# Two attention blocks on one core: value and output weights kept apart, keys for four pairs at once, and a new instruction order

## Chip, core and metric

The kernel runs on one core of a Trainium2 chip. The metric is the device time of one execution in microseconds (us), as the median of several executions. TensorE (PE), VectorE (DVE), ScalarE (ACT), GpSimd (POOL) and SyncE (SP, which issues the DMAs) each run their own instruction stream in order, and hand over to one another with semaphores.

## What is computed

`x` and the context `c` are 32 sequences of 64 tokens by 128 features. Block 0 has causal self-attention, cross-attention and a feed-forward layer, each followed by a layer norm, with 16 heads of width 8. Block 1 is cross-attention with 16 heads of width 64 and a given bias `f` that is added twice.

```python
def _mha(x, kv, Wq, Wk, Wv, mask, causal):       # block 0, width 8 per head
    energy = jnp.einsum('bhsk,bhtk->bhst', Q, K)
    lengths = jnp.sum(energy[:, :, 0, :] != 0, axis=-1)
    energy = jnp.where(cols >= lengths[:, :, None, None], -jnp.inf, energy)
    ...
    score = softmax(energy / sqrt(dk)); out = score @ V * m
# block 1, width 64 per head
qh, kh, vh = q @ wq + bq, c @ wk + bk, c @ wv + bv
weights = softmax(qh @ kh.T / 8 + f + f)
out = LN((weights @ vh) @ wo + bo + q)
```

## The kernel before

**Tiling.** Two sequences make a pair, 2 x 64 tokens on the 128 partitions, so there are 16 pairs. Each pair goes through three chains. Chain A is the self-attention and norm L1. Chain B is the cross-attention and norm L2, then the feed-forward layer and norm L3. Chain C is block 1 and norm L4. A works three or four pairs ahead of C and B two, so that in a full round all three chains have a pair in work.

**PSUM.** Each chain of block 0 has three banks: J (projections), E and X (scores, transposed weights, results). Chain C has two, `C.E[0]` and `C.E[1]`, through which everything of a pair passes in turn: transposed input, queries, scores, keys and values of a later pair, transposed weights, output, and then the input of the next pair.

**Chain C, step by step (before).** `C.x3t`/`C.x3ts` transpose and copy the input; `C.q_0/1` compute the queries in two halves of eight heads and `C.qs_0/1` (ACT, four instructions each) copy them out with bias and scale; `C.e` computes the scores (32 small matmuls); `C.fadd` (DVE) adds the bias `f`; `C.max` (DVE), `C.sub` (POOL), `C.exp` (ACT), `C.den` (DVE, sum and reciprocal) and `C.nrm` (DVE, the normalising product in place in `Pc`) are the softmax; `C.pt`/`C.pts` transpose and copy it; `C.o` multiplies by `VW` and `C.y` adds the residual. `C.k`/`C.ks` make the keys of one pair (8 matmuls 128x128; DVE adds the bias), and `C.v`/`C.vs` make the values. Before, the values are already multiplied by the output weights: at the start `C.fold` computes Wv[h] Wo[h] for all heads and splits it into two parts, so `C.v` is 12 matmuls of 512 columns in a faster number format (fp32r), and four DMAs (`C.vz`) bring the halves into place as `VW`.

**Chains A and B** have the same steps with their own names: `qkv`, `qk`, `q0`, `e0`, `nz`, `cnt`, `cut`, `kblk` (POOL, 128x1024), `e`, `max`, `sub`, `exp`, `pt`, `pts`, `pv`, `zts`, `z`, `zn`, `y`, `st`, `rstd` (POOL), `xh`, `gb` (POOL).

**Order.** A table written by hand, `TURN`, lists every step with the pair that it is ahead by. Each engine walks through the table once per round and issues the steps that are its own; the functions `run` and `body` do that. What an engine issues is thus fixed, and a step that waits holds up all that stands behind it on its engine. A full round does one pair of each chain.

Of the kernel before, what the change touches and what calls it, by code (L numbers as in the profile page):

```python
# [75 lines left out]
def bass_two_blocks(nc, consts, columns, x, xT, ctxn, ctxT, fs, Wq1, Wk1, Wv1, Wq2, Wk2, Wv2, fc1T, fc2T,  # L76
                    vecs, fc1b, wq, wk, wvT, wo, bq, bk, bv, out):
    with ExitStack() as stack:
# [23 lines left out]
        wvT_sb, wo_sb = sb("wvT_sb", [P, J, D]), sb("wo_sb", [P, J, D])  # L102
        wvo_hi, wvo_lo = sb("wvo_hi", [P, 2, 2, J // 2, D], F32R), sb("wvo_lo", [P, 2, 2, J // 2, D], F32R)
# [21 lines left out]
        def attention(name):  # L125
# [9 lines left out]
            a.V = [sb(name + f"_V{k}", [P, 2, H, SLOT]) for k in range(2)]  # L135
# [3 lines left out]
            a.zn = sb(name + "_zn", [P, D])  # L139
# [911 lines left out]
```

## Time and profile before

| | us |
|---|---|
| median of 3 runs | 418.62 (417.07 to 419.54) |
| the profiled execution, its own time | 419.26 |
| span of its instructions | 417.5 |
| busy in the span: PE, DVE, ACT, POOL | 367.7, 345.4, 225.9, 218.4 |

A profile row is one instruction, or several alike in a row: start, duration, engine, line of the kernel, operation, output <- inputs, count, and in brackets the idle time of the engine before it with what ended it. An fp32 matmul is recorded as two instructions, one for each pass over the moving columns. Since matmuls are pipelined, the duration of a record runs into the next one; what a group costs PE is the distance from its start to the start of the next group.

### The profile page before, as it was taken

Reading aid. Unit: us, or ns where it says so; the run is one execution under the profiler, and the core shown is the slowest. Engines: PE = TensorE matmul, PEld = TensorE weight load, DVE = VectorE, ACT = ScalarE, POOL = GpSimd, SP = SyncE. Lnnn points to the kernel's source line nnn. Section 1 sums busy time; section 2 is a strip of 40 time slices with the busy share of each in tenths; the row PEclk is TensorE's granted clock in tenths of the full one; section 3 lists DMA queues with packets and bytes.
Section 4 is the critical chain, followed back from the end, with each engine's and each line's share of the span. In section 5 each row is a group of like instructions: output and inputs, shape, how many; then the busy total and the mean of one; then the engine's idle time right before and its main releaser. Section 6 shows DMA issues by size and latency. Waiting matters only on the chain.

```text
span 417.5 us, 12301 instructions
## 1 busy us (share of the span) xinstructions
PE 367.7 (88%) x4816; PEld 282.1 (68%) x4816; DVE 345.4 (83%) x895; ACT 225.9 (54%) x549; POOL 218.4 (52%) x356
## 2 busy tenths in 40 slices
PE   2488779899999999999999999999999989998834
PEld 1355547677777786868686868686877767766633
DVE  3146586899999999999999999999999999695751
ACT  1022344666675666656665666576666575645431
POOL 0013244555747566565656565666575746554531
PEclk9999989999999999999999999999999999999996
DMA  6980000314141423224150504141414141414040
GB/s 193 308 328 2 2 0 16 88 52 105 58 102 58 95 61 82 80 54 108 27 134 9 128 33 104 59 103 58 103 59 104 57 104 60 102 58 102 6 104 13
DMA packets 15801, 34.61 MB, mean 83 GB/s; under 512 B 2560, under 2 KB 7936, under 8 KB 15616
## 3 DMA queue, kind: packets, MB, share of 16 engines
q1 hardware_dynamic: 15744, 33.83, 30.3%
q8 instruction: 38, 0.62, 0.7%
q14 instruction: 19, 0.16, 0.1%
HBM read 15.99 MB, written 1.05 MB: 41 GB/s over the span
## 4 chain that ended last, share of the span: by engine, by line
PE 47%; DVE 36%; issue 7%; ACT 3%; DMA 2%; POOL 2%; SPq 1%; POOLq 0%; DVEq 0%
DVE Pc L895 8%; PE C_E L509 7%; PE C_E L545 7%; PE C_E L521 4%; DVE denc L885 4%; PE A_E L386 4%; DVE kT L855 4%; DVE mxc L877 4%; DVE Sc L868 3%; PE C_E L532 2%; PE A_J L350 2%; DMA wo_sb<-in_wo 2%; PE B_E L419 2%; PE B_E L405 2%; PE C_E L315 2%
## 5 line engine op out<-in xcount | busy, mean ns | idle before, releaser
L938 POOL TENSOR_TENSOR L_ve<-L_mv,cst 128x1 f32<-128x1 f32 x64 | 12.1, 189 | 77.9 <-DVE L_mv L822 77.8
L949 POOL TENSOR_TENSOR L_xg<-L_xh,vec_sb 128x128 f32<-128x128 f32 x64 | 35.0, 547 | 32.2 <-DVE L_xh L831 32.2
L930 POOL TENSOR_TENSOR A_kblk<-A_qk,cst 128x1024 f32<-128x1024 f32 x16 | 30.3, 1896 | 34.1 <-DVE A_qk L755 34.1
L978 POOL TENSOR_TENSOR Sc<-Sc,mxc 128x512 f32<-128x512 f32 x32 | 33.4, 1043 | 24.0 <-DVE mxc L877 24.0
L643 ACT COPY vst<-C_E 128x512 f32<-128x512 f32 x64 | 37.6, 587 | 4.3 <-PE C_E L490 4.1
L657 ACT ACTIVATE qT<-C_E,bq 128x128 f32<-128x128 f32 x128 | 36.2, 366 | 5.6 <-PE C_E L509 5.6
L930 POOL TENSOR_TENSOR B_kblk<-B_qk,cst 128x1024 f32<-128x1024 f32 x16 | 30.4, 1897 | 15.5 <-DVE B_qk L755 15.5
L940 POOL TENSOR_TENSOR L_rstd<-L_ve,cst 128x1 f32<-128x1 f32 x64 | 35.1, 548 | 5.0
L509 PE MATMUL C_E<-x3T,wq_sb 128*128 128x128 f32 x256 | 36.8, 287 | 0.4 <-ACT x3T L649 0.4
L474 PE MATMUL C_E<-cTs,wk_sb 128*128 128x128 f32 x256 | 35.6, 282 | 1.3 <-DVE Sc L868 1.3
L895 DVE TENSOR_TENSOR Pc<-Pc,rdc 128x512 f32<-128x512 f32 x32 | 36.1, 1128 | 0.7
L545 PEld LDWEIGHTS C_E<-VW,PTc 128*64 128x64 f32 x512 | 29.0, 142 | 9.3 <-ACT PTc L674 8.9
L590 ACT ACTIVATE B_S<-B_S 128x512 f32<-128x512 f32 x32 | 20.2, 630 | 27.4 <-DVE B_S L789 26.9
L474 PEld LDWEIGHTS C_E<-cTs,wk_sb 128*128 128x128 f32 x256 | 31.0, 191 | 4.3 <-issue 2.6
L674 ACT COPY PTc<-C_E 128x512 f32<-128x512 f32 x32 | 18.4, 586 | 28.4 <-PE C_E L532 28.4
L509 PEld LDWEIGHTS C_E<-x3T,wq_sb 128*128 128x128 f32 x256 | 30.9, 191 | 4.1 <-ACT x3T L649 2.4
L545 PE MATMUL C_E<-VW,PTc 128*64 128x128 f32 x512 | 32.9, 284 | 0.7 <-ACT PTc L674 0.7
L532 PEld LDWEIGHTS C_E<-cst,Pc 128*128 128x128 f32 x128 | 14.1, 145 | 27.7 <-DVE Pc L895 18.0
L532 PE MATMUL C_E<-cst,Pc 128*128 128x128 f32 x128 | 21.2, 294 | 12.8 <-DVE Pc L895 12.3
L488 PE MATMUL C_E<-wvo_hi,cT_hi 128*128 128x512 f32 x64 | 29.2, 457 | 0.2 <-DVE kT L855 0.2
L868 DVE SCALAR_TENSOR_TENSOR Sc<-f,C_E 128x512 f32<-128x512 f32 x32 | 21.8, 681 | 8.0 <-PE C_E L521 8.0
L665 ACT ACTIVATE Pc<-Sc 128x512 f32<-128x512 f32 x32 | 20.4, 638 | 10.3 <-POOL Sc L978 10.3
(149 smaller groups left out, 1047.8 us busy)
## 6 DMA issues: line engine op xcount, KB each, us to landing
VW<-vst SPq DMA_DIRECT2D x64, 256.0 KB, 4.4
f<-in_fs SPq DMA_DIRECT2D x16, 512.0 KB, 3.5
cTs<-in_ctxT SPq DMA_DIRECT2D x1, 1024.0 KB, 6.6
out<-osb SPq DMA_DIRECT2D x16, 64.0 KB, 1.5
xTs<-in_xT SPq DMA_DIRECT2D x1, 960.0 KB, 8.3
vec_sb<-in_vecs SPq DMA_DIRECT2D x1, 640.0 KB, 4.3
wvT_sb<-in_wvT SPq DMA_DIRECT2D x1, 512.0 KB, 8.1
wo_sb<-in_wo SPq DMA_DIRECT2D x1, 512.0 KB, 9.3
```

The costliest lines, as they stand in the source:

```text
L474: last = mm(C.E[g][:, j * P:(j + 1) * P], wk_sb[:, c:c + P], cols(cTs, n), start=True, stop=True)
L509: last = mm(C.E[g][:, j * P:(j + 1) * P], wq_sb[:, c:c + P], x3T[:], start=True, stop=True)
L532: last = tr(C.E[g][:, j * P:(j + 1) * P], Pc[:, c:c + P], ident)
L545: last = mm(C.E[0][S * b:S * b + S, 0:D], PTc[:, c:c + S], VW[:, b, j], start=(j == 0), stop=(j == J - 1), skip_group_check=True)
L643: act.copy(vst[:, m // 2, 4 * (m % 2):4 * (m % 2) + 4].rearrange("p j d -> p (j d)"), C.E[m % 2][:, :]).then_inc(C.s_vs, 1)
L657: last = act.activation(qT[:, 4 * g + j], C.E[g][:, j * P:(j + 1) * P], ACT.Identity, bias=bq8[:, 4 * g + j:4 * g + j + 1], scale=float(DK ...
L868: dve.scalar_tensor_tensor(sc, f[n % 2][:, g * HALF:(g + 1) * HALF], 2.0, C.E[g][:, :], ALU.mult, ALU.add).then_inc(C.s_s, 1)
L895: tt(pr, pr, rdc[:, 8 * g:8 * g + 8].unsqueeze(2).to_broadcast([P, 8, S]), ALU.mult).then_inc(C.s_nrm, 1)
L930: tt(a.kblk[:], a.qk[:, 1].unsqueeze(1).to_broadcast([P, 8, P]), at["rmask"].unsqueeze(2).to_broadcast([P, 8, P]), ALU.mult).then_inc(a.s_ ...
L940: tt(l.rstd[:], l.ve[:], at["power"], ALU.pow).then_inc(l.s_rstd, 1)
L949: tt(l.xg[:], l.xh[:], l.g, ALU.mult).then_inc(l.s_xg, 1)
L978: tt(v, v, mxc[:, 8 * g:8 * g + 8].unsqueeze(2).to_broadcast([P, 8, S]), ALU.subtract).then_inc(C.s_sub, 1)
```

## The change

1. Wv and Wo are not folded. `C.fold`, its copies (`fhi`, `flo`), `C.chi` and `C.clo` and the four DMAs per pair are gone. `C.v` computes plain values in fp32 (4 matmuls with 64 stationary and 512 moving columns), ACT copies them with 2 instructions instead of 4. New steps: `C.zt` (32 matmuls 64x64x64: weights times values, transposed), `C.zts` (2 ACT copies of 128x512), and `C.o` (8 matmuls 128x128x128 with Wo).
2. Keys are computed for four pairs at once: `C.k` of pair n does two of the eight key blocks of a group of four pairs (2 matmuls with 512 moving columns), five rounds ahead. The bias is added by ACT (`C.ks`), not DVE.
3. In A and B each partition half keeps only the values of its own heads: the projection's value part has 64 columns instead of 128, and `v` on DVE becomes two narrow and two 64x128 instructions per pair and chain instead of one 128x32 and one 128x256.
4. `zn` and the sums `y` (L1, L2, L3, `ffn`) lie in PSUM. The score matmuls of the next pair therefore wait for `xh` of the pair before, no longer for `zn`; `B.tr` waits for L3's `xh`. `q0` and `cut` read PSUM.
5. `C.nrm` runs on POOL.
6. The loads at the start come in another order and in pieces (first four pairs of x and c, then the weights, then the rest). `C.bvo`, the product of Wo with the value bias, stands before the second `A.qkv` on PE.
7. `TURN` is a new table. (A table `SHIFT` that could delay single pairs holds zeros only.)

```diff
-                sp.dma_start(t[:], ap.rearrange("(j p) d -> p j d", p=P)).then_inc(w_fold, 16)
+            load_x(0, 0, FIRST)
...
+            sp.dma_start(wo_sb[:], wo.rearrange("(j p) d -> p j d", p=P)).then_inc(w_out, 16)
+            sp.dma_start(bv_sb[:], bv).then_inc(w_out, 16)
...
-                        sp.dma_start(VW[S * m:S * m + S, b], vst[S * b:S * b + S, m]).then_inc(C.s_vz, 16)
...
-            def energy(a, causal):
+            def energy(a, l, causal):
...
-                        pe.wait_ge(a.s_zn, 2 * n)
+                        pe.wait_ge(l.s_xh, n)
...
-                    for j in range(4):
-                        c = (4 * g + j) * P
-                        last = mm(C.E[g][:, j * P:(j + 1) * P], wk_sb[:, c:c + P], cols(cTs, n), start=True, stop=True)
+                    mm(C.E[g][:, :], wk_sb[:, j * P:(j + 1) * P], cTs[:, group * FIRST * P:(group + 1) * FIRST * P],
+                       start=True, stop=True).then_inc(C.s_k, 1)
...
-                    mm(bank[:, :], cT_hi[:], hi, start=True, stop=False)
-                    mm(bank[:, :], cT_hi[:], lo, start=False, stop=False)
-                    mm(bank[:, :], cT_lo[:], hi, start=False, stop=True).then_inc(C.s_v, 1)
+                    for r in range(2):
+                        last = mm(C.E[b][S * r:S * r + S, :], cTs[:, n * P + S * b:n * P + S * b + S], wv_sb[:, r],
+                                  start=True, stop=True)
...
+            def c_zt(n):
+
+                pe.wait_ge(C.s_pts, 2 * n + 2)
+                for jj in range(J // 2):
+                    for b in range(2):
+                        c = jj * P + S * b
+                        for hl in range(2):
+                            for r in range(2):
+                                k = slice(S * r, S * r + S)
+                                v = jj * P + DK1 * hl
+                                last = mm(C.E[r][DK1 * hl:DK1 * hl + DK1, c:c + S], V[n % 2][k, b, v:v + DK1],
+                                          PTc[k, hl * HALF + c:hl * HALF + c + S], start=True, stop=True)
...
+                    pe.wait_ge(C.s_zts, 2 * n + 1 + r)
+                    for jj in range(J // 2):
+                        last = mm(C.E[0][:, 0:D], zT[:, r, jj], wo_sb[:, 2 * jj + r], start=(r == jj == 0),
+                                  stop=(r == 1 and jj == J // 2 - 1))
...
-            def nrm(g):
-
-                def step(n):
-                    dve.wait_ge(C.s_rd, 2 * n + 1 + g)
...
+            def nrm(g):
+
+                def step(n):
+                    pool.wait_ge(C.s_rd, 2 * n + 1 + g)
+                    pr = heads(Pc[:, g * HALF:(g + 1) * HALF])
+                    tt(pr, pr, rdc[:, 8 * g:8 * g + 8].unsqueeze(2).to_broadcast([P, 8, S]),
+                       ALU.mult).then_inc(C.s_nrm, 1)
```

**PE at the start.** Before, from the first projection on; `wo_sb,wvT_sb` is the fold:

```order
L350 MATMUL A_J<-Wv_sb,xTs 64x128 x4
L315 MATMUL C_E<-wo_sb,wvT_sb 128x128 x4
L360 MATMUL A_J<-A_q,A_qk 64x16 x2
L315 MATMUL C_E<-wo_sb,wvT_sb 128x128 x4
L372 MATMUL A_J<-A_nz,ofb 128x16 x2
L374 MATMUL A_J<-ofb,A_nz 128x2
L315 MATMUL C_E<-wo_sb,wvT_sb 128x128 x4
L386 MATMUL A_E<-A_kblk,A_qk 64x512 x2
```

After:

```order
L326 MATMUL A_J<-Wv_sb,xTs 64x64 x4
L336 MATMUL A_J<-A_q,A_qk 64x16 x2
L348 MATMUL A_J<-A_nz,ofb 128x16 x2
L350 MATMUL A_J<-ofb,A_nz 128x2
L302 MATMUL C_E<-wo_sb,bv_sb 128x128 x8
L321 MATMUL A_J<-xTs,Wq_sb 128x128
L322 MATMUL A_J<-xTs,Wk_sb 128x128
L326 MATMUL A_J<-Wv_sb,xTs 64x64 x4
L362 MATMUL A_E<-A_kblk,A_qk 64x512 x2
```

The small steps of the first pair no longer stand behind the fold; the eight matmuls with `bv_sb` (before, in front of the third `A.qkv`) now stand in front of the second `A.qkv` and the first scores.

**PE in a full round, from the second half of the queries (`x3T,wq_sb`) to the scores (`kT,qT`) of chain C.** Before:

```order
L509 MATMUL C_E<-x3T,wq_sb 128x128 x4
L430 MATMUL B_X<-cst,B_zT 128x128 x2
L345 MATMUL A_J<-xTs,Wq_sb 128x128
L346 MATMUL A_J<-xTs,Wk_sb 128x128
L350 MATMUL A_J<-Wv_sb,xTs 64x128 x4
L442 MATMUL B_J<-cst,x_1 128x128
L443 MATMUL B_J<-cst,cm 128x128
L521 MATMUL C_E<-kT,qT 64x64 x32
```

After, with what follows the scores:

```order
L488 MATMUL C_E<-x3T,wq_sb 128x128 x4
L321 MATMUL B_J<-xc,Wq_sb 128x128
L322 MATMUL B_J<-xc,Wk_sb 128x128
L326 MATMUL B_J<-Wv_sb,xc 64x64 x4
L501 MATMUL C_E<-kT,qT 64x64 x32
L321 MATMUL A_J<-xTs,Wq_sb 128x128
L322 MATMUL A_J<-xTs,Wk_sb 128x128
L326 MATMUL A_J<-Wv_sb,xTs 64x64 x4
L336 MATMUL B_J<-B_q,B_qk 64x16 x2
L362 MATMUL A_E<-A_kblk,A_qk 64x512 x2
```

Less work stands between the queries and the scores, and the projection and the scores of chain A have moved behind the scores of chain C.

**POOL in a full round, around the softmax of chain C (`Sc,mxc` is `C.sub`).** Before:

```order
L978 TENSOR_TENSOR Sc<-Sc,mxc 128x512 x2
L930 TENSOR_TENSOR B_kblk<-B_qk,cst 128x1024
L949 TENSOR_TENSOR L_xg<-L_xh,vec_sb 128x128
L954 TENSOR_TENSOR osb<-L_xg,vec_sb 128x128
L930 TENSOR_TENSOR A_kblk<-A_qk,cst 128x1024
```

After:

```order
L932 TENSOR_TENSOR Sc<-Sc,mxc 128x512 x2
L891 TENSOR_TENSOR B_kblk<-B_qk,cst 128x1024
L941 TENSOR_TENSOR Pc<-Pc,rdc 128x512 x2
L910 TENSOR_TENSOR L_xg<-L_xh,vec_sb 128x128
L915 TENSOR_TENSOR x_1<-L_xg,vec_sb 128x128
```

The two normalising products stand directly behind `B.kblk`.

## Rows read from the trace of the kernel before

**Rows 1.** The page's chain that ended last: share of the span by engine.
```profile
PE 47%; DVE 36%; issue 7%; ACT 3%; DMA 2%; POOL 2%; SPq 1%; POOLq 0%; DVEq 0%
```
**Rows 2.** Busy time by engine in one full round: stretch, length, then each engine.
```profile
180.80:202.80 22.00, 21.38 (x299) 16.55 (x299) 21.09 (x56) 13.85 (x35) 13.66 (x22) 1.00 0.31 77
```
**Rows 3.** Timeline of PE in that round: start, duration, what.
```profile
181.43 0.65 PE L386 MATMUL A_E<-A_kblk,A_qk 64*64 64x512 f32 x2
...
182.34 0.38 PE L393 MATMUL A_E<-later,eye 64*64 64x512 bf16 x2
...
182.67 1.97 PE L545 MATMUL C_E<-VW,PTc 128*64 128x128 f32 x32
...
190.20 1.16 PE L521 MATMUL C_E<-kT,qT 64*64 64x64 f32 x64
191.29 0.49 PE L345 MATMUL B_J<-xc,Wq_sb 128*128 128x128 f32 x2
...
191.93 0.66 PE L350 MATMUL B_J<-Wv_sb,xc 128*64 128x128 f32 x8
192.52 1.16 PE L474 MATMUL C_E<-cTs,wk_sb 128*128 128x128 f32 x8
193.61 0.29 PE L360 MATMUL A_J<-A_q,A_qk 128*64 128x16 f32 x4
...
194.44 1.06 PE L474 MATMUL C_E<-cTs,wk_sb 128*128 128x128 f32 x8
195.34 0.60 PE L405 MATMUL A_X<-cst,A_S 128*128 128x128 f32 x4
...
195.86 0.48 PE L488 MATMUL C_E<-wvo_hi,cT_hi 128*128 128x512 f32 x1
...
197.35 0.23 PE L372 MATMUL A_J<-A_nz,ofb 128*128 128x16 bf16 x2
...
202.80 0.33 PE L532 MATMUL C_E<-cst,Pc 128*128 128x128 f32 x1 [0.57 <-DVE Pc L895]
```
**Rows 4.** Single lines over the whole run: count, duration ns min/median/max.
```profile
L895 DVE TENSOR_TENSOR Pc<-Pc,rdc x32: 681/1036/1480, 88.9 to 407.1; 128x512 f32<-128x512 f32 x32
...
L978 POOL TENSOR_TENSOR Sc<-Sc,mxc x32: 1038/1043/1048, 83.9 to 404.2; 128x512 f32<-128x512 f32 x32
```
**Rows 5.** The page's groups by line: busy us, mean ns | idle before them.
```profile
L930 POOL TENSOR_TENSOR B_kblk<-B_qk,cst 128x1024 f32<-128x1024 f32 x16 | 30.4, 1897 | 15.5 <-DVE B_qk L755 15.5
L643 ACT COPY vst<-C_E 128x512 f32<-128x512 f32 x64 | 37.6, 587 | 4.3 <-PE C_E L490 4.1
...
L868 DVE SCALAR_TENSOR_TENSOR Sc<-f,C_E 128x512 f32<-128x512 f32 x32 | 21.8, 681 | 8.0 <-PE C_E L521 8.0
```
**Rows 6.** Timeline of PE in a later round, chain A nearly done: queries to scores.
```profile
361.20 1.16 PE L509 MATMUL C_E<-x3T,wq_sb 128*128 128x128 f32 x8
362.20 0.39 PE L430 MATMUL B_X<-cst,B_zT 128*128 128x128 f32 x2
...
363.59 1.16 PE L521 MATMUL C_E<-kT,qT 64*64 64x64 f32 x64 [0.65 <-ACT qT L657]
```
**Rows 7.** Timeline of PE at the start.
```profile
16.47 2.07 PE L315 MATMUL C_E<-wo_sb,wvT_sb 64*128 64x128 f32 x8 [9.33 <-DMA wo_sb<-in_wo]
...
24.36 1.12 PE L386 MATMUL A_E<-A_kblk,A_qk 64*64 64x512 f32 x2
...
39.77 3.68 PE L326 MATMUL C_E<-wo_sb,bv_sb 128*128 128x128 f32 x16
43.28 0.39 PE L345 MATMUL A_J<-xTs,Wq_sb 128*128 128x128 f32 x2
```
**Rows 8.** Timeline of PE: queries of the first and the thirteenth pair; the last output.
```profile
76.23 1.16 PE L509 MATMUL C_E<-x3T,wq_sb 128*128 128x128 f32 x8
...
339.40 1.16 PE L509 MATMUL C_E<-x3T,wq_sb 128*128 128x128 f32 x8
...
408.90 3.38 PE L545 MATMUL C_E<-VW,PTc 128*64 128x128 f32 x32
```

More of the change, by code:

```diff
@@ L134, in attention @@
             a.S = sb(name + "_S", [P, H * S])
-            a.V = [sb(name + f"_V{k}", [P, 2, H, SLOT]) for k in range(2)]
+            a.V = [sb(name + f"_V{k}", [P, 2, J, 2, SLOT]) for k in range(2)]
             a.PT = sb(name + "_PT", [P, H * S])
@@ L224, in bass_two_blocks @@
         C.s_pts = sem("C_pts")
+        C.s_zt = sem("C_zt")
+        C.s_zts = sem("C_zts")
         C.s_o = sem("C_o")
@@ L231, in run @@
         def run(steps):
-            def body(i):
-                for chain, step, ahead in ORDER:
-                    fn = steps.get(chain + "." + step)
-                    n = i + ahead
-                    if fn and 0 <= n < PAIRS:
-                        fn(n)
-            for i in range(-AHEAD, PAIRS):
-                body(i)
+            for _, chain, step, n in PLAN:
+                fn = steps.get(chain + "." + step)
+                if fn:
+                    fn(n)
         def cols(t, n):
@@ L301, in _ @@
             mm, tr = nc.tensor.matmul, nc.tensor.transpose
-            def fold(part):
-                def step(n):
-                    if n:
-                        return
-                    hl, q = part // 2, part % 2
-                    if part == 0:
-                        pe.wait_ge(w_fold, 16 * 2)
-                    if part >= 2:
-                        pe.wait_ge(wvo_split, part - 1)
-                    r = slice(DK1 * hl, DK1 * hl + DK1)
-                    for j in range(4):
-                        last = mm(C.E[q][:, j * P:(j + 1) * P], wvT_sb[r, 4 * q + j], wo_sb[r, 4 * q + j],
-                                  start=True, stop=True)
-                    last.then_inc(wvo_ready, 1)
-                return step
             def bvo(n):
@@ L521, in c_e @@
                             last = mm(C.E[hl][S * b:S * b + S, j * S:(j + 1) * S], qT[r, j, S * b:S * b + S],
-                                      kT[r, j, S * b:S * b + S], start=True, stop=True)
+                                      keys[r, j, S * b:S * b + S], start=True, stop=True)
                 last.then_inc(C.s_e, 1)
@@ L1005 @@
-C.v_2+2 B.3xh+2 B.sub_1+3 A.pts_0+4 B.f2+2 A.z+4 A.y+4 A.pts_1+4 C.exp_0+1 C.v_3+2 C.gb+0 B.f3+2 C.vs_0+2
-C.fhi_3+4 C.exp_1+1 B.e+3 A.kblk+5 C.y+1 A.zts+4 B.f1s+2 A.st+4 C.pt_0+1 C.flo_3+4 C.pt_1+1 B.3rstd+2 C.vs_1+2
-C.fold_2+5 B.3gb+2 C.x3c+2 C.obias+3 C.st+1 A.rstd+4 B.f2s+2 C.flo_0+5 A.e+5
-"""
-ORDER = [(w[0], w[2:].split("+")[0], int(w.split("+")[1])) for w in TURN.split()]
-AHEAD = max(k for _, _, k in ORDER)
+B.pv_0+2 C.den_0+1 B.gb+2 C.qs_1+1 C.den_1+1 C.sub_0+1 A.sub_0+5 B.qk+3 B.pv_1+2 A.qk+6 C.ks_0+5 C.bvo+5 C.q_0+1
@@ new lines @@
+A.cnt+6 A.st+5 B.pts_0+3 B.pts_1+3 A.pt_1+5 C.gb+0 B.zn+3 B.y+3 C.zt+1 C.x3ts+2 B.st+3 B.q0+4 B.xts+4 C.xh+1
+A.pv_0+5 A.pv_1+5 B.pt_0+3 B.zts+3 A.xh+5 B.xh+3 C.o_0+1 C.o_1+1 C.rstd+1 C.fadd_0+2 A.rstd+5 B.pt_1+3 C.max_0+2
+B.nz+4 B.tr+4 C.obias+6 C.loadf+5 B.rstd+3 C.qs_0+2 A.z+5 C.fadd_1+2 C.max_1+2 C.store+4 B.cut+4 A.max_0+6
+C.x3t+2 A.q0+7 B.v+4
+"""
+SHIFT = """
+A 0 0 0 0 0 0 0 0 0 0 0 0 0 0 0 0
+B 0 0 0 0 0 0 0 0 0 0 0 0 0 0 0 0
+C 0 0 0 0 0 0 0 0 0 0 0 0 0 0 0 0
+"""
+WORDS = TURN.split()
@@ L1012 @@
+LATER = {r[0]: [float(v) for v in r[1:].split()] for r in SHIFT.strip().split("\n")}
+PLAN = sorted((n + k / len(WORDS) - int(w.split("+")[1]) + LATER[w[0]][n], w[0], w[2:].split("+")[0], n)
+              for k, w in enumerate(WORDS) for n in range(PAIRS))
 _OUT = ((B, S, D), "float32")
```

350 lines of the change are left out of this document (158 added, 192 removed).

## Prediction

> **What bounds the kernel now.** I read the chain of waits first. It is nearly all PE and DVE, with POOL at 2% and DMA at 2% [rows 1], so neither engine alone sets the end: work goes back and forth between the two. The busy times of one full round say how close both are to their limit: PE 21.4 us and DVE 21.1 of 22.0, ACT 13.9, POOL 13.7 [rows 2]. The queries of the first pair start on PE at 76.23 us and those of the thirteenth at 339.40 [rows 8], so twelve full rounds take 263.2 us, 21.93 each. What is left is the head (76.2 us) and the tail (417.5 - 339.4 = 78.1 us). In a full round PE stands still in one place for 0.57 us, before the second half of the transposed weights, and it is DVE's normalising product that releases it (the last of [rows 3]). PE's own work is thus 21.93 - 0.57 = 21.36 us per round. This is the number that the change has to lower; relief on DVE alone is worth at most the 0.57.
>
> **The full round, part by part (PE, from start to start).**
>
> Keys: before 1.09 + 0.90 = 1.99 us (192.52 to 193.61 and 194.44 to 195.34 in [rows 3]). The price of an fp32 matmul with 512 moving columns is that of the score matmuls of chain A, where four tiles stream side by side, each two passes, in 182.34 - 181.43 = 0.91 us. Two of them are 1.82: -0.2.
>
> Values: six of the twelve fp32r matmuls take 197.35 - 195.86 = 1.49 us, so all twelve some 3.0. After there are four fp32 matmuls of 512 columns, two and two side by side in the column halves: 2 x 0.91 = 1.8, so -1.2. If the two didn't overlap it would be 3.6, +0.6 (a rival, below). That narrow tiles do overlap is shown by the output product: 32 records of 128 columns in 1.9 us are 59 ns each, and the keys, the same columns over the full width, need 1.09/8 = 136 ns.
>
> Value part of the projections in A and B: 192.52 - 191.93 = 0.59 us each for 128 columns; half the columns, -0.3 each, -0.6 (nothing, if the 64 columns were bounded by something else).
>
> New `C.zt`: 32 matmuls of 64x64x64 in four tiles, like the scores of chain C, 191.29 - 190.20 = 1.09: +1.1. `C.o`: before 1.9; after eight matmuls of 128 columns, priced as queries (four in 1.00, [rows 6]) or keys (four in 1.09): 2.1, +0.2.
>
> The sum is -0.2 - 1.2 - 0.6 + 1.1 + 0.2 = -0.7, PE's work becomes 20.7 us (20.4 to 21.3 with terms at their milder ends, leaving out the rival).
>
> DVE loses the two key copies and the two products (0.68 and a mean of 1.13 us each by their lines, 3.6 per round) and gets some 0.4 for the split value steps: about 17.9 us. It drops well below PE, and that cost is hidden. ACT loses two copies of 0.59 [rows 5], the small cast, and gains two key copies and two `zts`: about +1, 15 us, hidden by its 8 us of idleness as a sum, not at each place. The four DMAs per pair land early and nobody on the chain waits for them; nothing.
>
> **Where PE waits now.** Two places, both new. (a) Between the second half of the queries and the scores of C, ACT must finish eight small copies. In a round where PE has too little else, the scores start 363.59 - 361.20 = 2.39 us after that half starts, 0.65 of it waited [rows 6]. The new order leaves the projection of B between them: 1.09 + (191.29 to 192.52, 1.23, less 0.3) = 2.0 us. So PE waits 0.4. (b) Transposed weights: from the end of the scores DVE does two additions and two maxima at 0.68 and one small step (2.9 us), then POOL in its order one more subtraction at 1.04, `B.kblk` at 1.90 and two products. A product on POOL has the form and size of the subtraction, min 1038 and max 1048 ns [rows 4]: 2.1. That is 7.9 us to the release. Meanwhile PE has the projection and scores of A (0.9 + 1.2), keys and values (3.6), the scores of B (0.9), small groups (an estimate, 0.9) and the first transposes (0.6): 8.1. It just fits, with 0.2 to spare. The longer hold of the banks in A and B (the scores wait for `xh`) costs nothing: on DVE `xh` stands just ahead of C's additions, so it is done when C's scores end; A's next scores stand 1.1 us later on PE, B's about 6. So the round is 20.7 + 0.4 = 21.1 us, and twelve of them give 12 x (21.1 - 21.93) = **-10.0 us**. What is late next is (a), a handful of ACT copies, and directly behind it (b).
>
> A rule that speaks against (b): [rows 4] show the product on DVE at 0.68 us alone and 1.48 us at worst, beside POOL, and POOL's 512-wide subtraction at 1.04 whatever DVE does. The Trainium skill, GPSIMD Engine Reference, section 3.1, gives an fp32 `tensor_tensor` on GpSimd as 1.96 times slower than on DVE; that would make each product 1.3 us, use up the spare time and lengthen the round by 0.4, 5 us over twelve rounds. The trace's 1.04 is for the same shape and is what I take. The same skill, SBUF — State Buffer, "Who interferes with whom", says that a DVE instruction with two SBUF inputs contends with GpSimd; moving the product away ends this for DVE's largest such instruction, and the 0.68 against 1.48 agrees.
>
> **Head.** Before, PE waited until 16.47 us for `wo_sb` and ran four fold groups of 2.07 each; the first scores stood at 24.36 [rows 7]. After, the same wait holds `bvo`, which is now second in line, and `wo_sb` stands behind more bytes and more DMA issues: I take 19 us (16.5 to 21). Then 3.6 for `bvo` and some 2.3 for a projection at the slow rate (twice its 1.2) give 25 for the first scores, +0.7. The 3.5 us of `bvo` at 39.77 to 43.28 are gone from there. PE ran its matmuls slowly until 43.28: a pair of score records takes 1.12 us at 24.36 and 0.65 in the full round [rows 7, 3]; right behind `bvo` it ran at the full rate (0.39 for two projection records). If `bvo` brings that about at 25 already, the pieces of 20 us that follow are shorter, some 4 us; the three rounds of the head are set by latency, not by PE's sum, so I count 1. The head is **-3.7 us** (-8 to +3).
>
> **Tail.** With A gone, the path of one pair through C sets the pace. It gets `zt` (1.1) and a copy (0.6, the second one is hidden by the first output matmuls) for four pairs, 4 x 1.7 = 6.8, and for the last pair at the slow rate 1.1 more (the last output at 408.90 took 3.38, not 1.9 [rows 8]). Against that, the keys have left the last three rounds (2.0 each on PE) and the values are shorter (I count 0.4 of their 1.2): 3 x 2.4 = 7.2. **+0.7 us** (-4 to +5).
>
> Sum: -10.0 - 3.7 + 0.7 = -13.0. The profiled execution took 419.26 us with a span of 417.5; so 406.3 for it, and 405.6 against the median of 418.62. I say 406.
>
> **Rivals.**
>
> R1, slower: POOL becomes the pacemaker of the round. All that stands behind `B.kblk` is released by it, and there is only 0.2 us to spare. If a product on POOL takes twice the 1.04, in conflict with DVE as DVE's did (rows 4: 681 to 1480 ns for one instruction), the round is 21.1 + 2.1 - 0.2 = 23.0: 12 x 1.07 - 3 = +10, about **428 us**. It decides from a round of 22.2, that is from 1.7 us per product. Against it: the POOL rows don't vary. 12%.
>
> R2, the same: the two value matmuls of a half don't overlap, or a wait of one us arises on ACT (its queue puts key copies before the exponentials). Round 22.0, head -3: **416 us**. 10%.
>
> R3, more: PE runs at its full rate from the first 25 us, which takes 8 us from the head, and (a) doesn't bind, so that the round is PE's 20.7 or less: -8 - 15 + 1 = -22, **397 us**. 17%.
>
> R4, less: the loads keep `bvo` to 21 us or beyond and the deeper staging of A before B makes the head 3 us longer; the round is right: **412 us**. 15%.
>
> My own sum, 401 to 410: 46%. Faster by over 0.5% (which is about what a measurement of this kernel can tell from no change, 2 us) is then 46 + 17 + 15 and a part of R2: 0.80; the same 0.07; slower 0.13. The range leaves out R1 and the end of R3: 394 to 419.
>
> **What the profile after would show.** Distance of the first query matmuls from pair to pair: 21.1; over 22 refutes the sum. PE's work per group: keys and values 1.8 each, `zt` 1.1, `o` 2.1. POOL's product at 1.04, and PE's wait before the transposes under 0.2 us; a wait of over 1 us released by POOL is R1. PE's idle time before the scores of C 0.4, released by ACT. At the start `bvo` at 19 us and the first scores of A at 25, the first queries of C at 72 to 73. DVE busy at most 18 us per round. The prediction is wrong if ACT or POOL show up in the chain of waits with more than a few per cent.

## The result, and the profile after

| us | before | after |
|---|---|---|
| median (20 executions each) | 417.67 | 415.00 |
| lowest to highest | 413.48 to 419.64 | 412.68 to 417.83 |
| the profiled execution, its span | 419.26, 417.5 | 412.68, 410.8 |
| busy: PE, DVE, ACT, POOL | 367.7, 345.4, 225.9, 218.4 | 347.7, 309.3, 235.4, 236.2 |

The ratio of the times is 0.9933, with a 95% interval of 0.9907 to 0.9958. The change makes the kernel 2.7 us faster; 13 were forecast. The profiled execution of after is the fastest of its 20, that of before is 1.6 us slower than its median, so the two traces differ by 6.7 us where the medians differ by 2.7.

The page's chain that ended last, after, for [rows 1]:

```profile
PE 65%; ACT 15%; DVE 8%; issue 4%; POOL 3%; SPq 3%; DMA 2%; POOLq 0%; DVEq 0%
```

PE has taken DVE's place. A full round is as [rows 2] show it for before. Busy time by engine, then the granted clock, from the queries of one pair to those of the next:

```profile
179.39:200.38 20.99, 20.50 (x337) 14.47 (x331) 19.44 (x59) 14.44 (x36) 14.73 (x25) 1.00 0.09 30
```

The same round on PE's timeline, for [rows 3]; one wait is left in it, before the scores of C:

```profile
181.50 0.39 PE L321 MATMUL B_J<-xc,Wq_sb 128*128 128x128 f32 x2
...
182.90 1.16 PE L501 MATMUL C_E<-kT,qT 64*64 64x64 f32 x64 [0.40 <-ACT qT L644]
183.99 0.49 PE L321 MATMUL A_J<-xTs,Wq_sb 128*128 128x128 f32 x2
...
186.42 1.96 PE L453 MATMUL C_E<-cTs,wk_sb 128*128 128x512 f32 x4
188.32 1.08 PE L467 MATMUL C_E<-wv_sb,cTs 128*64 128x512 f32 x4
189.43 0.30 PE L426 MATMUL B_J<-cst,x 128*128 128x128 f32 x1
...
189.80 1.06 PE L467 MATMUL C_E<-wv_sb,cTs 128*64 128x512 f32 x4
190.79 0.65 PE L362 MATMUL B_E<-B_kblk,B_qk 64*64 64x512 f32 x2
...
192.13 1.04 PE L512 MATMUL C_E<-cst,Pc 128*128 128x128 f32 x8
...
194.52 1.16 PE L526 MATMUL C_E<-PTc,C_V 64*64 64x64 f32 x64
195.62 0.69 PE L395 MATMUL A_E<-A_PT,A_V 128*32 128x64 f32 x32
...
196.73 1.95 PE L535 MATMUL C_E<-wo_sb,C_zT 128*128 128x128 f32 x16
198.52 0.60 PE L381 MATMUL B_X<-cst,B_S 128*128 128x128 f32 x4
```

Keys take 1.90 us, the values 1.11 and 0.99, `zt` 1.10 and `o` 1.79. POOL in the same round: the products follow `B.kblk`, and the second ends at 192.40, while the eight transposes start at 192.13, so that their second half starts about 0.2 us behind it:

```profile
188.12 1.90 POOL L891 TENSOR_TENSOR B_kblk<-B_qk,cst 128x1024 f32<-128x1024 f32 x1
190.36 2.04 POOL L941 TENSOR_TENSOR Pc<-Pc,rdc 128x512 f32<-128x512 f32 x2 [0.34 <-DVE rdc L859]
```

By stages, from the queries of the first and the thirteenth pair ([rows 8] for before; after they start at 74.43 and 325.97):

| us | before | forecast | after, profiled | difference |
|---|---|---|---|---|
| head | 76.2 | -3.7 | 74.4 | -1.8 |
| twelve rounds | 263.2 | -10.0 | 251.5 | -11.6 |
| tail | 78.1 | +0.7 | 84.8 | +6.7 |

The tail alone takes back more than half of what the rounds give. The page's clock row of after shows where; a slice is 10.3 us, and the digits below 9 all stand in the last eight slices, from 329 us on:

```profile
PEclk9999999999999999999999999999999978999866
```

In windows of 10 us, columns as in [rows 2]:

```profile
330.00:340.00 10.00, 6.80 (x70) 2.31 (x63) 7.01 (x19) 2.48 (x5) 7.71 (x9) 0.73 0.17 54
...
350.00:360.00 10.00, 6.36 (x105) 3.24 (x105) 7.75 (x22) 4.04 (x11) 7.11 (x9) 1.00 0.17 54
...
390.00:400.00 10.00, 3.73 (x88) 2.80 (x82) 4.43 (x8) 2.43 (x4) 5.45 (x7) 0.63 0.02 7
400.00:410.00 10.00, 4.94 (x60) 4.45 (x53) 1.11 (x4) 1.07 (x2) 1.64 (x4) 0.67 0.03 8
```

Before had 1.00 in every such window from 330 to 400 us. PE's timeline of after tells what it did: it waited, and the groups behind the waits ran at the lower of the clock's two levels, 1.2 and not 2.4 GHz.

```profile
332.37 0.23 PE L348 MATMUL B_J<-B_nz,ofb 128*128 128x16 bf16 x2 [1.51 <-DVE B_nz L719]
335.31 0.45 PE L426 MATMUL B_J<-cst,x 128*128 128x128 f32 x1 [1.70 <-DVE B_V L752]
...
380.22 1.99 PE L526 MATMUL C_E<-PTc,C_V 64*64 64x64 f32 x64 [0.25 <-ACT PTc L661]
...
396.06 1.11 PE L512 MATMUL C_E<-cst,Pc 128*128 128x128 f32 x4 [5.39 <-POOL Pc L941]
...
399.17 1.99 PE L526 MATMUL C_E<-PTc,C_V 64*64 64x64 f32 x64 [0.68 <-ACT PTc L661]
401.86 3.79 PE L535 MATMUL C_E<-wo_sb,C_zT 128*128 128x128 f32 x16 [0.70 <-ACT C_zT L631]
```

By their rows `zt` takes 1.99 and not 1.16, `o` 3.79 and not 1.95 as in the full round.

### The profile page after: what moved, and what is told of

It is laid out like the page before. It is cut to its first block, busy times and chain, and to the rows that moved or that the text cites. A ratio compares the mean times of both kernels' runs of the same rounds, so it can differ in the third digit from the quotient of the medians.

```text
span 410.8 us, 13138 instructions
## 1 busy us (share of the span) xinstructions
PE 347.7 (85%) x5296; PEld 242.4 (59%) x5296; DVE 309.3 (75%) x897; ACT 235.4 (57%) x561; POOL 236.2 (57%) x372
## 4 chain that ended last, share of the span: by engine, by line
PE 65%; ACT 15%; DVE 8%; issue 4%; POOL 3%; SPq 3%; DMA 2%; POOLq 0%; DVEq 0%
ACT qT L644 8%; PE C_E L535 8%; PE C_E L453 6%; PE C_E L467 6%; PE C_E L526 5%; PE C_E L488 4%; PE C_E L501 4%; PE A_E L362 4%; PE B_E L362 3%; PE B_E L395 3%; ACT A_S L566 2%; PE C_E L512 2%; PE A_X L381 2%; ACT PTc L661 2%; PE A_E L395 2%
## 5 line engine op out<-in xcount | busy, mean ns | idle before, releaser
L559 ACT COPY A_qk<-A_J 128x256 f32<-128x256 f32 x16 | 6.0, 372 | 71.8 <-PE A_X L369 67.0
L467 PE MATMUL C_E<-wv_sb,cTs 128*64 128x512 f32 x128 | 35.2, 628 | 0.8 <-DVE Sc L840 0.8
L941 POOL TENSOR_TENSOR Pc<-Pc,rdc 128x512 f32<-128x512 f32 x32 | 32.8, 1042 | 5.3 <-DVE rdc L859 5.3
L535 PE MATMUL C_E<-wo_sb,C_zT 128*128 128x128 f32 x256 | 33.3, 286 | 1.6 <-ACT C_zT L631 1.4
L535 PEld LDWEIGHTS C_E<-wo_sb,C_zT 128*128 128x128 f32 x256 | 31.5, 200 | 2.5 <-ACT C_zT L631 2.5
L453 PE MATMUL C_E<-cTs,wk_sb 128*128 128x512 f32 x64 | 31.4, 614 | 0.0
L612 ACT ACTIVATE kT<-C_E,bk_sb 128x512 f32<-128x512 f32 x32 | 21.9, 683 | 15.0 <-PE C_E L453 15.0
L501 PE MATMUL C_E<-kT,qT 64*64 64x64 f32 x1024 | 18.6, 221 | 8.2 <-ACT qT L644 8.2
L622 ACT COPY C_V<-C_E 128x512 f32<-128x512 f32 x32 | 18.5, 583 | 10.8 <-PE C_E L467 10.8
L857 DVE TENSOR_REDUCE denc<-Pc 128x8 f32<-128x512 f32 x32 | 21.2, 663 | 2.2 <-ACT Pc L652 1.8
```

The costliest lines, as they stand in the source:

```text
L453: mm(C.E[g][:, :], wk_sb[:, j * P:(j + 1) * P], cTs[:, group * FIRST * P:(group + 1) * FIRST * P], start=True, stop=True).then_inc(C.s_k, 1)
L467: last = mm(C.E[b][S * r:S * r + S, :], cTs[:, n * P + S * b:n * P + S * b + S], wv_sb[:, r], start=True, stop=True)
L501: last = mm(C.E[hl][S * b:S * b + S, j * S:(j + 1) * S], qT[r, j, S * b:S * b + S], keys[r, j, S * b:S * b + S], start=True, stop=True)
L535: last = mm(C.E[0][:, 0:D], zT[:, r, jj], wo_sb[:, 2 * jj + r], start=(r == jj == 0), stop=(r == 1 and jj == J // 2 - 1))
L941: tt(pr, pr, rdc[:, 8 * g:8 * g + 8].unsqueeze(2).to_broadcast([P, 8, S]), ALU.mult).then_inc(C.s_nrm, 1)
```

## The experiments

All times are medians. Before was measured beside every group of runs and took 417.69, 417.87 and 417.93; a ratio is that to before, with its interval. A difference to after is one to its second median, 415.70. To fill PE's waits the runs use filler matmuls: work whose result nobody reads.

### The tail's clock

**Fillers in the tail.** The definition, and one of the seven places:

```diff
+            def fill(count):
+                for _ in range(count):
+                    mm(A.E[:, :], A.nz[:], eye64[:, :].unsqueeze(1).to_broadcast([P, 8, S]), start=True, stop=True)
...
+                    if n == 15 and g == 0:
+                        fill(21)
                     pe.wait_ge(C.s_nrm, 2 * n + 1 + g)
```

> The kernel after, with idle time of PE in the tail filled by matmuls that nobody reads (bf16, eye64 against A.nz into the free bank A.E, 0.2 us each): 6 before `B.cnt` and 5 before `C.e` of the last two pairs, 7 before `B.f1` of pairs 13 and 14, 10 before `B.f2`, 21 before the first transposes of the last weights, 2 before the last `zt`, 2 before each of the last `o`. In after the granted clock is 0.73 in the stretch from 330 to 340 us and 0.63 and 0.67 in the last 20 us, and groups at the low level take 1.8 to 2 times as long (values 1.98 instead of 1.08, zt 1.99 instead of 1.09, o 3.79 instead of 1.79). Theory (the low clock in the waits of the tail is a real part of its length): clock above 0.9 in these stretches, tail from the queries of the thirteenth pair to the end 84.8 - 4 to 6 us, total 3 to 6 us below the kernel after. Rival (the tail is bounded by the hand-overs between DVE, POOL and ACT, the slow groups only fill what would be waits): the clock rises but the total stays within 1 us, or grows by what the fillers cost where they don't quite fit.

409.11 us, ratio 0.9818 (0.977 to 0.9866). The tail takes 405.9 - 327.57 = 78.3 us, 6.5 less. The two windows that stood at 0.73 and 0.63:

```profile
330.00:340.00 10.00, 9.38 (x118) 4.31 (x116) 8.01 (x22) 3.97 (x11) 7.39 (x9) 1.00 0.17 54
390.00:400.00 10.00, 8.18 (x104) 4.85 (x103) 3.29 (x7) 3.50 (x6) 5.45 (x7) 1.00 0.03 9
```

There is more work on PE, and the tail is shorter. The rival, that slow groups only fill what would be waits, is refuted.

**After, unchanged, once more.**

> The kernel after, unchanged, on the chip and in the hour of the three runs beside it. The earlier loads gave 407.5 us by median and a span of 406.0, the fillers 409.1 and 405.9, y and zn in SBUF 410.6 and 410.1, against a median of 415.0 and a profiled span of 410.8 of the kernel after in another hour. If its median is 415 again (413.5 to 416.5), these differences are the edits' own, and the profiled execution of after (412.68, the fastest of 20) is an unusually short one. If it is 412 to 413, some 2.5 us of each difference is a matter of the chip or the hour, and y and zn in SBUF gain at most 2 us.

415.70 us (12 executions), ratio 0.9959 (0.9928 to 0.999), so the differences of the edits are their own. The profiled execution is a long one this time, span 415.8. Rounds (251.7) and tail (84.8) are those of the first profile, but the first queries stand at 79.25, not 74.43, and the clock tells why. The same three windows of the head, in this profile:

```profile
30.00:40.00 10.00, 6.88 (x71) 3.75 (x72) 5.27 (x17) 2.42 (x5) 3.55 (x5) 0.78 0.04 16
40.00:50.00 10.00, 8.71 (x70) 5.17 (x69) 5.33 (x18) 5.06 (x10) 2.27 (x3) 0.67 0.00 1
50.00:60.00 10.00, 8.32 (x77) 4.03 (x80) 7.17 (x19) 4.20 (x8) 3.14 (x4) 0.87 0.01 2
```

In the first profile they read 1.00. The waits are the same in both, and the groups are longer; the scores of A for the second pair stand at 35.90 with 0.65 us there, and here:

```profile
36.52 1.11 PE L362 MATMUL A_E<-A_kblk,A_qk 64*64 64x512 f32 x2 [2.38 <-DVE L_xh L811]
```

So two executions of one kernel differ in the head by 5 us, by the clock alone. The first profile is the rarer case: of the first 20 executions three had its mean granted clock of 0.969 and took 412.7 us, the other 17 had 0.952 to 0.965 and took 413.1 to 417.8. With the rounds and the tail as in both profiles, the median span of these 12 executions (413.9) leaves 77.4 us for the head of a typical one; that is worked out, not seen.

**Fillers in the last two pairs of before** (3 and 5 before `C.e`, 20 before the last transposes, 2 before the last `C.o`; the form is the same).

> The kernel before, with the same sort of filler matmuls in PE's waits of its last two pairs: 3 and 5 before `C.e`, 20 before the last transposes, 2 before the last output product. Before lost its clock only there (0.75 and 0.73 after 400 us), after lost it from 330 us on. Theory (the tail of after fails by the clock, that of before hardly did): before gains 1.5 to 3 us in all, since only the last transposes (1.1 to 0.65) and the last output product (3.4 to 1.9) are on the path at the low level, where the fillers gave 6 us to after; with the clock held in both, the tails differ by the term of the prediction, +0.7, to within 2 us. Rival (fillers give the same in both, so that the clock doesn't explain the difference of the two tails): before gains 5 us or more.

416.40 us, ratio 0.997 (0.9933 to 1.0008), so the medians alone can't tell it from no change. The tail is 410.5 - 333.86 = 76.6 us against 78.1, which is 1.5 less, as expected. With the clock held in both, the tails are 76.6 and 78.3, so the work and waits of the change cost 1.7 us there. Its profiled execution had its first queries at 70.47, those of before in [rows 8] 76.23, with not one filler in the head, so the head of before varies in the same way. The waits are the same up to there, but PE leaves its low level with the fourth fold group, where [rows 7] have it until 43.28:

```profile
27.00 1.16 PE L319 MATMUL C_E<-wo_sb,wvT_sb 64*128 64x128 f32 x8
...
70.47 1.16 PE L513 MATMUL C_E<-x3T,wq_sb 128*128 128x128 f32 x8
```

The stage table above thus compares a slow head of before with a fast one of after. The median span of before in its 23 executions beside these runs is 416.1; less the rounds (263.2) and the tail (78.1) that leaves 74.8 us, against the 77.4 of after. For typical executions the head did not get shorter by 1.8 us but longer by 2.6. This too is worked out, not seen.

**The clock held at both ends of after.**

```diff
+                early_fill(A.E, 45)
                 pe.wait_ge(w_out, 16 * 2)
...
+                    if a is A and n in (1, 2):
+                        early_fill(A.E, 9 if n == 1 else 4)
                     pe.wait_ge(a.s_kblk, n + 1)
```

> The kernel after with fillers at both ends and nothing else changed: those of the tail as before, and at the start 45 in front of `bvo` (PE waits 11.9 us for bv_sb there), 9 and 4 in front of the scores of chain A of pairs 1 and 2 (waits of 2.37 and 1.06 us for the norm). The second profile of after showed the clock at 0.78, 0.67 and 0.87 in the three stretches from 30 to 60 us and its first queries at 79.25; the first profile showed it at 1.0 there and 74.43. Theory (the prediction's working is right where it is a matter of work and waits, and the missing 9 us are the clock at both ends): first queries at 74 to 75.5, clock 1.0, rounds 20.99, tail 78, span 404 to 406 in all executions, 406 to 408 us of device time. Rival (the waits at the start don't cost the clock, it falls for another reason): head 77 to 80 in most executions, a median of 409 as with the tail's fillers alone.

405.22 us, ratio 0.9707 (0.9668 to 0.9746), a little below what I expected. First queries at 73.43, twelve rounds 251.5, tail 78.3, and the mean granted clock is 1.00. Against after this is 10.5 us less, 6.6 by the tail's fillers alone and 3.9 more by those of the head. `bvo` now runs at the full rate:

```profile
21.05 2.05 PE L311 MATMUL C_E<-wo_sb,bv_sb 128*128 128x128 f32 x16
```

### The head

**Loads of wo_sb and bv_sb first.**

```diff
+            sp.dma_start(wo_sb[:], wo.rearrange("(j p) d -> p j d", p=P)).then_inc(w_out, 16)
+            sp.dma_start(bv_sb[:], bv).then_inc(w_out, 16)
             load_x(0, 0, FIRST)
...
-            sp.dma_start(wo_sb[:], wo.rearrange("(j p) d -> p j d", p=P)).then_inc(w_out, 16)
-            sp.dma_start(bv_sb[:], bv).then_inc(w_out, 16)
```

> The kernel after, with the loads of wo_sb and bv_sb issued before the bulk loads of x, context and weights instead of behind them. In the kernel after PE stands still from 8.5 to 20.4 us, in front of the eight matmuls of `bvo`, until bv_sb has landed (issued at 12.59, landed 7.8 us later). Theory: the head misses its gain because of this one wait; with the loads ahead, `bvo` starts at 9 to 12 us, the first scores of A come 8 to 10 us earlier (15 to 17 instead of 24.9), and the first queries of C at 66 to 69 us instead of 74.4; the total is 5 to 9 us below the kernel after, some 407 to 410 by medians. Rival: the head is paced by latency further back (the context and x land later now, the rounds of the head wait for DVE and ACT): the first scores move, the first queries move by less than 2 us, and the total stays within 1 us.

407.54 us, ratio 0.9787 (0.9739 to 0.9834), 8.2 less than after. PE's timeline at the start, in after:

```profile
20.40 3.71 PE L302 MATMUL C_E<-wo_sb,bv_sb 128*128 128x128 f32 x16 [11.88 <-DMA bv_sb<-in_bv]
...
24.86 0.65 PE L362 MATMUL A_E<-A_kblk,A_qk 64*64 64x512 f32 x2
```

And with the early loads:

```profile
8.56 3.79 PE L302 MATMUL C_E<-wo_sb,bv_sb 128*128 128x128 f32 x16 [0.20 <-DMA bv_sb<-in_bv]
...
13.76 1.07 PE L362 MATMUL A_E<-A_kblk,A_qk 64*64 64x512 f32 x2
...
31.16 3.78 PE L453 MATMUL C_E<-cTs,wk_sb 128*128 128x512 f32 x4
```

The scores come 11 us earlier, the first queries (70.35) only 4 before the 74.43 of the first profile, just outside what I expected, and 7 before the 77.4 of a typical execution. The granted clock is 0.84 and 0.74 between 20 and 40 us, and the keys take 3.78 and not 1.98 us.

**y and zn of A and B in SBUF, scores waiting for `zn`** (most of part 4 undone).

```diff
-            a.y, a.zn = a.X[:, 2 * P:3 * P], a.X[:, 3 * P:4 * P]
+            a.y, a.zn = sb(name + "_y", [P, D])[:], sb(name + "_zn", [P, D])[:]
...
-                        pe.wait_ge(l.s_xh, n)
+                        pe.wait_ge(a.s_zn, 2 * n)
```

> The kernel after, with `zn` and the sum `y` of chains A and B in SBUF again, and the scores of the next pair waiting for `zn` again and not for `xh`; L3's sum and `ffn` stay in PSUM. It undoes most of part 4. Theory of the prediction (the longer hold of the banks costs nothing, and the place of these 128-column sums is indifferent to PE): full round 20.9 to 21.1 us, total within 1 us of the kernel after. Rival 1 (PSUM operands relieve DVE of its contention with GpSimd): DVE's small steps in the norms get longer, round or tail grow, total 1 to 4 us above. Rival 2 (the hold of the banks costs time in the tail, where B's scores follow directly on its norm): total 1 to 3 us below.

410.58 us, ratio 0.9856 (0.9801 to 0.9912), 5.1 less than after, more than either rival said. Rounds (21.00) and tail (83.9) are nearly those of after, so the gain must be at the start. Its own profile doesn't show it as a number: the first queries stand at 74.56, against 74.43 in after's first, with the clock at 0.66 from 30 to 40 us where that one had 1.00. What it shows is the wait that is gone. The scores of A for the second pair wait for the norm of the first, in after:

```profile
35.90 0.65 PE L362 MATMUL A_E<-A_kblk,A_qk 64*64 64x512 f32 x2 [2.37 <-DVE L_xh L811]
```

The same scores in this kernel, which wait for nothing, although they run at the low level:

```profile
35.57 1.12 PE L362 MATMUL A_E<-A_kblk,A_qk 64*64 64x512 f32 x2
```

**All three together:** early loads, fillers in the tail, y in SBUF.

> The kernel after with three edits together: the early loads of wo_sb and bv_sb, the fillers in the tail, and y and zn of A and B in SBUF. They act in different stretches: head, tail and (if anywhere) the norms. Theory (independent terms): first queries at 70 us, rounds of 20.99, tail of 78 from the thirteenth queries to the end, so a span of 70.4 + 251.7 + 78.3 = 400.4 and 402 us of device time, or less if y in SBUF has a gain of its own (its medians say 4, its trace says 0 to 1). Rival: the terms overlap (the early loads already raised a part of what the fillers raise) and the total stays above 404.

395.63 us, ratio 0.9489 (0.9446 to 0.9532). First queries at 62.94, rounds 251.7, tail 78.3. This is below before by 22 us and below after by 20, and below the 402 that I expected. The three gains by medians (8.2, 6.6 and 5.1) add up to it.

**The same without y in SBUF.**

> The kernel after with the early loads of wo_sb and bv_sb and the fillers of the tail, and without y and zn in SBUF: it tells what those were worth in the combination of all three, 395.6 us. There the scores of chain A of pair 1 waited for nothing, while with y and zn in PSUM they wait 2.3 us for `xh`. Theory (part 4 costs the head its waits for `xh`, at most 2.3 + 1.1 us and what the clock loses by them): first queries at 66 to 70 us instead of 62.9, total 398 to 402. Rival (y in SBUF gains in the round or the tail, or not at all): first queries at 63 us.

401.57 us, ratio 0.9605 (0.9569 to 0.9641), so undoing part 4 is worth 5.9 us here; first queries at 67.19 and not 62.94, with both waits back:

```profile
27.24 1.12 PE L368 MATMUL A_E<-A_kblk,A_qk 64*64 64x512 f32 x2 [2.37 <-DVE L_xh L829]
...
39.82 0.65 PE L368 MATMUL A_E<-A_kblk,A_qk 64*64 64x512 f32 x2 [1.07 <-DVE L_xh L829]
```

**All three, with fillers in the head** (9 before the scores of A of pairs 1 to 3, 9 before the first keys).

> As the run before, with filler matmuls at the start too: 9 before the scores of chain A of pairs 1 to 3 (the waits of 2.3 us there, released by the norm), 9 before the first keys (a wait of 2.1 us for `obias`). With the early loads alone the granted clock fell to 0.84 and 0.74 in the stretches 20 to 40 us, and the keys at 31.16 took 3.8 us, not 1.9; that is why the first scores moved by 10 us and the first queries only by 4. Theory: clock 1.0 from 20 us on, first queries at 66 to 68 us, total 2 to 4 us below the run before. Rival (the head is set by the latency of the norm of chain A, 11 to 13 us per pair, and not by PE): first queries still at 70, total the same to within 1 us.

402.26 us, ratio 0.9644 (0.9602 to 0.9686), 6.6 slower where I expected 2 to 4 faster. With `zn` in SBUF the scores of A have no wait to fill, so each of the three groups of fillers there (2.1 us) lies on the path; the first queries stand at 69.68. The clock had been 1.00 there without them.

**All three, `C.obias` behind two maxima of A on DVE** (the parts of `TURN` that change).

```diff
-B.nz+4 B.tr+4 C.obias+6 C.loadf+5
+B.nz+4 B.tr+4 C.loadf+5
...
-A.max_1+5 A.nz+6
+A.max_1+5 C.obias+5 A.nz+6
```

> The combination of three with one step moved in the table: `C.obias` on DVE stands behind the first two maxima of chain A instead of ahead of them. In the combination DVE stands in `C.obias` until 17.5 us for vec_sb, with the scores of A lying ready since 15.2, and PE waits 3.03 us in front of the first keys. Theory: the maxima and the exponentials of pair 0 go ahead, the first transposes come right behind the keys (19.9 instead of 21.1), the head shortens by 1 to 3 us, total 393 to 395. Rival (the keys' own load wk_sb, bk_sb and bq_sb lands at 17 us and the rest of the head hides the gain): within 1 us of 395.6.

397.04 us, ratio 0.9492 (0.9457 to 0.9527), so there is no gain. PE waits for `obias` 3.17 us, where it waited 3.03, until 17.61. The rival of the expectation is nearer, though the time is 1.4 us above 395.63 and not within 1.

### The full round

**The products on DVE again** (part 5 undone; each directly behind its `C.den`).

> The kernel after, with the two normalising products of chain C back on DVE, each directly behind the sum and reciprocal that it needs. It prices part 5 of the change. By the trace of after DVE is busy 17 to 18 us of a round of 20.97, so two products of 0.68 to 1.1 us lift it to about 19.5, still under PE; the weights of C are then ready earlier. Theory (part 5 is neutral in the full round, since PE waits for ACT in front of the scores and not for POOL): the round stays at 20.9 to 21.2 us; in the tail the last pair gets its weights 1 to 3 us earlier, since there PE waits 5.4 us for POOL's product; total 0 to 3 us below the kernel after. Rival (the move to GpSimd is what makes the round fit): DVE delays the A and B steps, the round is 21.5 us or more and the total 5 us or more above the kernel after.

434.81 us, ratio 1.0445 (1.0389 to 1.0502), 19 slower than after. A round takes 22.5 us. Its busy times:

```profile
186.69:209.17 22.48, 20.89 (x335) 14.47 (x330) 20.86 (x61) 14.46 (x36) 13.04 (x23) 1.00 0.09 28
```

DVE is busy for 20.86 of 22.48, and the chain's shares are PE 38%, DVE 36%, ACT 13%. With the products on DVE the chain goes between it and PE again, as in before. The move to POOL is what makes this order fit, and not neutral as I expected; only this one place on DVE was tried. My expectation had also read DVE too low, at 17 to 18 us of a round of after, where it is busy for 18.7 to 19.4.

**All three together, with `A.qkv` in front of `C.e`** (the part of `TURN` that changes).

```diff
-C.exp_0+1 C.e+1 A.max_1+5 A.nz+6 A.qkv+6 C.ks_1+5
+C.exp_0+1 A.qkv+6 C.e+1 A.max_1+5 A.nz+6 C.ks_1+5
```

> The combination of three with `A.qkv` moved in front of `C.e` on PE: then 0.95 us more of work stands between the queries and the scores of chain C, and the wait of 0.40 us for ACT's copies there, the only one that the full round has left, is covered. It tells what is late next. Theory of the prediction (behind the wait for ACT there is 0.2 us to spare before the transposed weights wait for POOL): PE's wait of 0.40 goes, the scores come 0.55 us later, PE waits 0.3 to 0.4 for POOL's product instead, and the round stays at 20.9 to 21.0. Rival (the place before the transposes has more to spare): the round falls to 20.6, twelve rounds give 4.8 us, total 391.

401.83 us, ratio 0.9614 (0.9582 to 0.9647), 6.2 slower than without it, against both theories. The wait of 0.40 is gone, and the round is 21.53. PE's waits between 100 and 290 us, all of them (line waited at, releaser, sum, times, longest):

```profile
PE B_J L434 <- issue: 4.6, 8, 0.6
PE B_J L354 <- DVE B_nz L737: 2.4, 9, 0.3
```

The transposes behind POOL's products don't wait. What is late next are the small steps of chain B: on DVE `B.nz`, `B.cut` and `B.v` stand behind the additions and maxima of C, which now start later, and `B.cnt` and `B.f1` on PE need them (L434 is `B.f1`, which waits for `B.v` and `B.cut`). The profile names no releaser for it ("issue"), so this is inferred; one round of DVE agrees, where the values of B end at 204.19 and `B.f1` starts at 204.29.

```profile
203.58 0.61 DVE L770 TENSOR_TENSOR B_V<-B_J,B_V 64x128 f32<-64x128 f32 x2
```

On PE, in the same round:

```profile
204.29 0.30 PE L434 MATMUL B_J<-cst,x 128*128 128x128 f32 x1 [0.57 <-issue]
```

## Why the prediction was wrong

**The round was right.** 21.1 us were forecast, 20.97 measured, which makes the gain of twelve rounds 11.6 and not 10.0. Keys at 1.8 measured 1.90, values 1.8 measured 2.10, `zt` 1.1 and 1.10, `o` 2.1 and 1.79; PE is busy for 20.5 where I had 20.7. Wait (a) is 0.40 us, released by ACT, to the digit. POOL's product is 1.04 (the rows of its 32 instructions run from 1040 to 1044 ns), and its place (b) has about 0.2 us to spare. R1 and R2 are refuted; that R2's 416 us is nearest to the measured 415.0 says nothing for it, since its round was 22.0. The Trainium skill, GPSIMD Engine Reference, section 3.1, would have had 1.96 times DVE's time, measured there on a larger instruction; the trace has 1.04 against 0.69, which is 1.5 times, and the measurement decides. What I expected behind (a) was wrong: `B.nz` and `B.f1` come before (b).

**DVE's relief was too large.** I forecast 17.9 us per round. It is 18.7 to 18.9 in eight of the eleven full rounds, and 19.3 to 19.4 in three, of which the round shown is one. The products and key copies are gone, but the split value steps cost 1.12 us per chain where one 128x256 and one narrow instruction took 0.67, so 0.9 and not 0.4 per pair, and `xh`, where it reads its input from PSUM, takes 0.40 us and not 0.34. The rest of the difference was not looked for. It stayed hidden; the run with the products on DVE shows how little room there is.

**The tail is the step that failed.** "+0.7 (-4 to +5)" measured +6.7. I priced the tail's groups at the full rate and gave the low one to the last pair's `zt` alone. That was wrong because the same edit that takes work off PE in the tail (A's lead, keys computed five rounds ahead) makes it wait 1.5 and 1.7 us at a time from 330 us on, and there the granted clock falls to 0.73. With the waits filled the tail is 78.3 us, +0.2 against [rows 8], and +1.7 against before with its own clock held. So the term of work and waits was right to 1 us, and a term for the clock, 6.5 us in after and 1.5 in before, was missing.

**The head failed as well, in its sign.** -3.7 was forecast (its terms, +0.7, -3.5 and -1, add up to -3.8); the two profiles give -1.8, but typical executions +2.6 as worked out above. `bvo` was to start at 19 and started at 20.40, first scores at 25 and 24.86, the queries at 72.5 and 74.43, in the first profile. Two terms were wrong. The first is the clock again, which falls there in most executions of after: 3.9 us, by the fillers. I had seen PE run slowly until 43.28 in before and counted a gain of 1 us from an early `bvo`; with the fillers in its tail before reached the full rate at 27.00, with `bvo` at 35.67, so the level in this stretch is not given by where `bvo` stands. The second is "the longer hold of the banks costs nothing". It was argued for the full round, where it holds; in the head, where one pair of A follows directly on another, the scores wait 2.37 and 1.06 us for `xh`, where before waited 0.90 for `zn`, and the reversal is worth 4 us of head and 5 to 6 of the total.

**What the near hit with a held clock says.** With fillers in both its ends after takes 405.2 us, and 406.0 was forecast. That is luck, since the forecast was taken from a before that loses time to its clock as well. The two profiles with the fullest clocks are better compared: before with fillers in its tail (head 70.5, rounds 263.4, tail 76.6, span 410.5) and after with the clock held (73.4, 251.5, 78.3, 403.2).

| us | forecast | fullest clocks |
|---|---|---|
| head | -3.7 | +3.0 |
| twelve rounds | -10.0 | -11.9 |
| tail | +0.7 | +1.6 |
| sum | -13.0 | -7.3 |

So work and waits give some 7 us and not 13, and the head is where they were mis-sized. The +3.0 is a lower bound, since this head of before still ran at the low level until 27.00. The 4.6 us between 7.3 and the 2.7 measured are what the clock costs after more than before, as far as two profiles tell. Of the rivals R4 had this head (3 us longer with a right round), though not for its first reason, since `bvo` started at 20.40 and not at 21 or beyond. One of R3's conditions, PE at its full rate from 25 us, was met in the first profile without the 8 us that it promised.

The Trainium skill, TensorE: Matmul & The Clock Gate, Part 1, puts the penalty of the slow ramp at a kernel's start under 1% of a typical span. For the ramp the runs agree: `bvo` takes 3.71 us in after and 2.05 behind fillers, 1.7 of 410.8. What cost more here are the later falls, in the head again and in the tail; with them the fillers give back 10.5 of 415.7 us, 2.5%.

The prediction named POOL or ACT in the chain as a sign of error. ACT is there with 15%, and that sign was itself wrong: wait (a), which it forecast, puts eight ACT copies into every round of the chain.

**Left open:** what a fall of the clock needs. In the head the same kernel holds it in one execution and loses it in the next; no run tells why. In the tail the same two waits, of 1.5 and 1.7 us, stand before 332 and 335 us, where the clock fell, and before 354 and 357 us, where it read 1.00. Before with a held clock in its head wasn't tried, so how much of its own 417.7 us is clock is not known beyond the 5.8 us by which its two profiled heads differ.

## What to carry to other kernels

Price the stretches where PE waits on small steps at both levels of its clock, and reckon that work taken off PE there can come back as clock: here the tail lost 6.5 us to it, where before lost 1.5. Filler matmuls in the true waits of the tail gave 6.6 us; in front of steps that had no wait they cost their full length. Before a stage is compared, ask how far it varies between executions: one profile of each kernel had the head shorter by 1.8 us, where typical executions had it longer. An argument that a wait is covered holds for the stretch it was made for: look at the pipeline's fill and drain again, where the neighbouring chain's work isn't there to cover it.

## What the hardware showed

PE's busy share in a window doesn't order the clocks: in after it is 6.80 of 10 us at a granted clock of 0.73 (330 to 340 us) and 6.36 at 1.00 (350 to 360 us). Two executions of one program had their first queries at 74.43 and 79.25 us, with clocks of 1.00 and 0.67 to 0.87 from 30 to 60 us.

At the start the clock column doesn't tell the level, and the groups' lengths do. In before it reads 1.00 in every window from 20 to 50 us, though the score records take 1.12 us at 24.36 and `bvo` 3.68 us at 39.77; the level is the low one until 43.28.

DVE's 128x512 product took 681 to 1480 ns in before ([rows 4]), and what POOL ran beside it decides. It took 1.03 or 1.04 us where `B.kblk` (128x1024) overlapped it for 0.49 us, 1.47 or 1.48 where `A.kblk` did for 0.92 (1.28 for 0.73, once), and 0.68 or 0.69 where neither did. With the products back on DVE in after, it took 0.94 in the two cases with 0.40 us of `B.kblk`, and otherwise 0.69 to 0.76, although POOL's 128x128 products lay beside it for up to 0.7 us. On POOL the product takes 1040 to 1044 ns.
